# Adaptive-norm FFN on one core: the first token tile in quarters on two queues, fewer matmuls on ones, and one token tile of the second pass two chunks earlier

## What is computed

```python
# x: (32, 64, 1024) f32; weights: (16, 64, 64); w1: (1024, 4096); w2: (4096, 1024)
W = weights[condition]                              # one 64x64 matrix for each of 32 rows
t = einsum('bct,bcd->bdt', x, W)                    # conditioned input, (32, 64, 1024)
h = gelu(einsum('bsd,df->bsf', t, w1) + b1)         # tanh form
out = x + einsum('bsf,fd->bsd', h, w2) + b2
```

## Time and profile before

| | us |
|---|---|
| median of 3 runs (lowest, highest) | 1261.19 (1260.48, 1261.66) |
| the profiled execution | 1260.64 |
| its span | 1258.8 |
| TensorE busy (matmuls) | 1253.7 |
| VectorE busy | 825.6 |
| ScalarE busy | 566.9 |
| GpSimd busy | 188.1 |

### The profile page before, as it was taken

The page is one execution under the profiler, slowest core; times in us unless marked ns, Lnnn a source line. Parts: engine busy times, 40 slices in busy tenths (PEclk is TensorE's granted clock), DMA queues, the critical chain, the costliest instruction groups (busy, mean ns, idle before and its releaser), DMA issues.

```text
span 1258.8 us, 15370 instructions
## 1 busy us (share of the span) xinstructions
PE 1253.7 (100%) x5664; PEld 1043.1 (83%) x5664; DVE 825.6 (66%) x1087; ACT 566.9 (45%) x969; POOL 188.1 (15%) x95
## 2 busy tenths in 40 slices
PE   9999999999999999999999999999999999999998
PEld 9888888888888888888888888888888888888887
DVE  5977787676577777657655455554547767784764
ACT  4845454454544444444434444444444444444442
POOL 4362223321000000000034233312200000000000
PEclk9999999999999999999999999999999999999999
DMA  9586655764997322349835224544189932223431
GB/s 343 160 275 244 242 196 222 283 250 177 384 392 283 97 89 99 101 165 360 310 137 195 95 119 174 184 184 145 74 330 396 351 132 93 101 101 100 155 131 51
DMA packets 94090, 249.28 MB, mean 198 GB/s; under 512 B 7328, under 2 KB 15552, under 8 KB 92608
## 3 DMA queue, kind: packets, MB, share of 16 engines
q1 hardware_dynamic: 93408, 248.14, 54.6%
q10 hardware_dynamic: 576, 0.15, 0.1%
q0 software_dynamic: 32, 0.00, 0.0%
HBM read 162.28 MB, written 85.98 MB: 197 GB/s over the span
## 4 chain that ended last, share of the span: by engine, by line
PE 97%; DVE 1%; DMA 1%; SPq 0%; POOL 0%; ACT 0%; issue 0%; ACTq 0%; DVEq 0%
PE ps L580 48%; PE ps L564 48%; DMA w_raw<-in_L_ffn_inter_w_dram 1%; PE ps L517 1%; POOL s_w L476 0%; SPq L321 0%; DVE y_whole L795 0%; DVE acc L878 0%; DVE lhs L800 0%; DVE y_whole L782 0%; DVE y L789 0%; SPq L318 0%; ACT lhs L646 0%; ACT y_stage L623 0%; SPq L317 0%
## 5 line engine op out<-in xcount | busy, mean ns | idle before, releaser
L564 PE MATMUL ps<-y,lhs 128*128 128x512 f32 x2688 | 611.4, 389 | 0.0
L580 PE MATMUL ps<-rhs,lhs 128*128 128x512 f32 x2688 | 609.6, 389 | 0.0
L580 PEld LDWEIGHTS ps<-rhs,lhs 128*128 128x128 f32 x2688 | 504.7, 188 | 104.6
L564 PEld LDWEIGHTS ps<-y,lhs 128*128 128x128 f32 x2688 | 504.2, 188 | 104.3
L716 ACT ACTIVATE lhs<-h_raw 128x512 fp32r<-128x512 f32 x224 | 141.6, 632 | 345.8 <-PE ps L580 340.2
L859 DVE TENSOR_TENSOR lhs<-h_raw,lhs 128x512 fp32r<-128x512 f32 x224 | 155.0, 692 | 188.5 <-ACT lhs L716 188.5
L800 DVE TENSOR_TENSOR lhs<-w_raw,lhs 128x512 fp32r<-128x512 f32 x128 | 111.1, 870 | 131.6 <-ACT lhs L646 131.5
L646 ACT ACTIVATE lhs<-w_raw 128x512 fp32r<-128x512 f32 x128 | 80.9, 633 | 171.7 <-PE ps L564 165.2
L862 DVE TENSOR_TENSOR rhs<-W,rhs 128x512 fp32r<-128x512 f32 x224 | 153.3, 684 | 0.0
L800 DVE TENSOR_TENSOR lhs<-s_w,lhs 128x512 fp32r<-128x512 f32 x96 | 91.3, 953 | 89.3 <-ACT lhs L646 89.1
L468 POOL TENSOR_TENSOR s_w<-w_raw 128x1024 f32<-128x1024 f32 x16 | 48.9, 3055 | 620.3 <-PE ps L580 354.0
(11 more groups left out here) (38 smaller groups left out, 290.1 us busy)
## 6 DMA issues: line engine op xcount, KB each, us to landing
h_raw<-h_mem SPq DMA_DIRECT2D x112, 512.0 KB, 3.3
w_raw<-in_L_ffn_inter_w_dram SPq DMA_DIRECT2D x32, 1024.0 KB, 8.6
h_mem<-hs SPq DMA_DIRECT2D x64, 512.0 KB, 4.5
W<-in_L_ffn_output_w_dram SPq DMA_DIRECT2D x32, 1024.0 KB, 12.4
h_mem<-c SPq DMA_DIRECT2D x48, 512.0 KB, 5.4
y_mem<-y_out SPq DMA_DIRECT2D x28, 512.0 KB, 3.5
y<-y_mem SPq DMA_DIRECT2D x7, 2048.0 KB, 12.8
acc<-in_x_dram SPq DMA_DIRECT2D x16, 512.0 KB, 9.0
```

The lines of the kernel that those rows point to most:

```text
L564: last = nc.tensor.matmul(ps[:, bank, :], w[:, k, :], y[i][:, part, k, :], start=(i in FRESH and k == 0 and u == 0), stop=(k == KH - 1 and ...
L580: last = nc.tensor.matmul(ps[:, bank2(h, j, tb), :], lhs[s % RING][:, a, blk(tb)], rhs[r][:, w, :], start=(j in FRESH and q == 0 and u == ...
```

## The change

Three things. The first token tile is loaded in four quarters of 256 columns instead of two halves of 512: quarters 0 and 2 are issued by SyncE, 1 and 3 by ScalarE ahead of b1, and TensorE waits for a quarter before every second of the tile's eight matmuls. `WARM` is 13 instead of 15. The eighth token tile of the second pass (j = 7) is multiplied behind chunk 7 instead of chunk 9, and so ScalarE copies it out at chunk 10 instead of 12.

```diff
-    WARM = 15
+    WARM = 13
-        x0_half = sem("x0_half")
+        x0_quarter = [sem(f"x0_quarter{i}") for i in range(4)]
+        def quarter(i):
+            return slice(i * D // 4, (i + 1) * D // 4)
-        BEHIND = (1, 1, 3, 3, 5, 5, 7, 9)
+        BEHIND = (1, 1, 3, 3, 5, 5, 7, 7)
-            sp.dma_start(x0[:, 0, 0:BANK], x_tok[0, :, 0, 0:BANK]).then_inc(x0_half, 16)
-            sp.dma_start(x0[:, 0, BANK:D], x_tok[0, :, 0, BANK:D]).then_inc(x0_in[0], 16)
+            for i in (0, 2):
+                sp.dma_start(x0[:, 0, quarter(i)], x_tok[0, :, 0, quarter(i)]).then_inc(x0_quarter[i], 16)
-                    pe.wait_ge(x0_in[j] if j else x0_half, 16)
+                    if j > 0:
+                        pe.wait_ge(x0_in[j], 16)
-                        if j == 0 and kb == KH:
-                            pe.wait_ge(x0_in[0], 16)
+                        if j == 0 and kb % 2 == 0:
+                            pe.wait_ge(x0_quarter[kb // 2], 16)
             act.dma_start(cond_all[:, SETS // 2:SETS], cond_sets[:, SETS // 2:SETS]).then_inc(cond_in, 16)
+            for i in (1, 3):
+                act.dma_start(x0[:, 0, quarter(i)], x_tok[0, :, 0, quarter(i)]).then_inc(x0_quarter[i], 16)
             act.dma_start(b1_rows[0:F // P], b1.rearrange("(a p) -> a p", p=P)).then_inc(b1_in, 16)
```

## The result

| | us |
|---|---|
| kernel before, median of 6 runs (lowest, highest) | 1261.07 (1260.48, 1261.71) |
| changed kernel, median of 6 runs (lowest, highest) | 1270.81 (1269.45, 1272.01) |
| ratio, with 95% interval | 1.0077 (1.0064 to 1.0089) |
| profiled execution of the changed kernel, its span | 1270.26, 1268.5 |

The change makes the kernel 9.7 us slower, 0.8%. In the profiled executions the spans differ by the same 9.7 us. The result is near the upper end of my range (1264.7 to 1271.0), 2.6 us above the forecast of 1268.2, and close to the first rival, which had the clock fall.

What follows compares the result with a forecast made beforehand. TensorE was taken to bound the kernel. Part 1 counted zero; gaps of 1.83 and 5.18 us before chunks 11 and 12 summed to 7.0, giving 1268.2 us against the median, range 1264.7 to 1271.0.

Steps and rivals of the forecast that it cites:

- first rival: TensorE's clock falls in the new gap, costing 1.7 us more, 1270 in all; chance 0.24.
- Where the time lies: TensorE alone bounds the kernel after 36.79 us; any gap opened there is paid in full.
- Part 1 is zero: Start: quartered first token tile and two fewer matmuls on ones gain nothing; w1 landing moves -0.4 to +0.4 us.
- tile 1 takes a sooner start away: Start: tile 1 has 0.03 us of slack, so a sooner tile 0 is waited away there.
- The wait on the staging store: ScalarE before tile 7's copy: idle some 5.7 us until tile 5's staging DMA lands, copy starting at 64.41.
- The two gaps: TensorE before chunks 11 and 12: 1.83 and 5.18 us lost, 7.0 in sum.
- the row at 93 us: Where both queue, GpSimd's sum goes ahead of VectorE's operation, as at 92.85 and 93.36; VectorE's took 2.88 us.
- The clock: TensorE behind the new gaps: the forecast left the clock unmoved; its fall, priced at 1.7 us, was a rival at 0.24.
- Tile 7's move on TensorE is a pure exchange: Chunks 8 and 9 come 1.7 us later, chunk 10 begins at 63.90 as before, and TensorE waits for nothing.

Runs made afterwards that it cites:

- late copy: The changed kernel with tile 7's matmuls behind chunk 7 but its ScalarE copy at chunk 12 as before; 1264.5 us, ratio 1.0021.
- y6 early: The changed kernel with VectorE making second-pass tile 6's low part before, not behind, its low part for chunk 11; 1262.39 us, ratio 1.0012.
- part 2 alone: The kernel before with only tile 7 of the second pass moved behind chunk 7; 1269.28 us, ratio 1.0065.
- kernel whose clock was held: The changed kernel with 20 idle matmuls, computing nothing used, on TensorE before chunk 12; 1267.7 us, ratio 1.0057.
- later sums: The changed kernel with GpSimd's first sum for w1 group 1 waiting for VectorE's low part for chunk 12; 1266.54 us, ratio 1.0054.
- 10 idle matmuls: The changed kernel with 10 matmuls that compute nothing used on TensorE before chunk 12; 1268.94 us, ratio 1.0067.

## Why the prediction was right, and where it was off

**Where the time lies: right.** TensorE bounds the kernel after 36.8 us, and a gap there is paid in full. The spans differ by what the gaps and the clock make up.

**Part 1 is zero: right in the sum, wrong in the details.** I let tile 0 begin 0 to 0.6 us sooner. In the changed kernel it began at 6.86, not 6.55: 26 records on ones took 5.82 us where 30 had taken 5.16, because the ones ran longer at the slow pace in that execution. In others of this study the 26 took from 4.59 to 5.92. SyncE's first quarter landed 5.0 us after its issue at 1.57, at 6.57, no sooner than the half tile. Nor does tile 0 wait for x and the ones alone, as my working had it: in the late copy and with y6 early it waited 0.4 and 0.5 us for GpSimd's copy into `wdiag`. In the changed kernel nothing of it reached the first stage: chunk 0 began at 21.08, before at 21.05. That tile 1 takes a sooner start away, as I had said, shows in part 2 alone:

```profile
8.75 12.77 PE L500 MATMUL ps<-wdiag,x 128*128 128x128 f32 x112 [0.45 <-DMA x<-in_x_dram]
```

Tile 0 had begun at 6.27 there. In the changed kernel it began late, and TensorE had no wait at tile 1.

**The wait on the staging store: right.** Forecast 64.41, measured 64.56; the store took 8.3 us. Storing it ahead of the load took the whole loss away. ScalarE stood still for 6.15 us where I had some 5.7.

**The two gaps: right.** Forecast 1.8 and 5.2, measured 2.2 and 5.0, sum 7.0 against 7.3; 6.8 by the kernel whose clock was held. GpSimd's sums went ahead of both halves of y6, as I took from the row at 93 us.

**The clock: the step that failed.** I gave the first rival 0.24 and the forecast, with the clock unmoved, 0.50. The clock fell in the profiled execution, and the mean clock of each of the six runs was 0.996 or 0.997 where the kernel before has 1.0. Its price was mis-sized as well: 1.7 us, from the start, against 2.7 to 2.9. Behind the gap TensorE was busy at the lower level for 5.5 us and lost half. The start was a poor measure for that: it scatters, since the 26 records took 4.59 to 5.92 us where 26 x 0.114 = 3.0 would do, 1.6 to 3.0 us more; and it can be read from the pace of the records only, since the granted clock reads 1.00 there in both traces. Of the Trainium skill's rule (TensorE: Matmul & The Clock Gate, HAM oscillation) that waiting brings the clock down, I said that the fall would come in some executions. For the gap of 4.8 us it came in all six. So the 9.7 us are two gaps that I had right and a fall of the clock that I had left to a rival; the range held because it reached as far as that rival.

**Tile 7's move on TensorE is a pure exchange: wrong.** The late copy showed that chunks 8 and 9 coming 1.7 us later leave so little room that y6 can meet GpSimd's sums, and the median goes up by 3 us. In the changed kernel the split for chunk 11 waits longer still for ScalarE, so the forecast didn't suffer.

## What to carry to other kernels

Before moving a step earlier on an engine that works in order, look at the wait that ended last before that step in the trace, and ask whether what it waits for moves too. If it doesn't, everything queued behind the step waits in its stead. Look also at what the delayed work will run beside. Here 6 us of a stalled engine with much spare time cost some 2 us by themselves (an estimate: 1.5 us late in the kernel with later sums, which had 0.8 us less to lose), some 5 more through the sums of GpSimd, and 2.7 more by the clock. A transfer that a wait hangs on belongs ahead of a large load in the same queue: here it landed in 3.9 us ahead of the load and in 8.3 behind it, and issuing the load one store later took the whole loss away.

## What the runs showed of the hardware

TensorE's clock fell to 1.2 GHz (granted 0.50) behind gaps much shorter than the 4.8 us of the changed kernel. In the profiled executions it fell behind gaps of 2.0 us and again 3.2 us (part 2 alone), 2.1 us (y6 early) and 2.55 us (10 idle matmuls). It did not fall behind 2.07 us (the changed kernel's first gap), 2.78 us (the late copy) and 3.13 us (the later sums):

```profile
83.00:86.00 3.00, 3.00 (x13) 1.00 1.02 320
```

The same kernel can go either way: with the late copy and with the later sums the mean clock was 1.0 in some runs and 0.997 to 0.999 in others, and with y6 early it fell in one run of ten. What decides the runs don't show. It stayed low for 3 to 7 us each time.

A 512-column operation of VectorE on two operands in SBUF took 0.68 us alone and 1.3 to 2.4 us where a sum of GpSimd held it. Where both had work queued, GpSimd's sum went first in the changed kernel, and two operations of VectorE beside two sums took 6.69 us and not 2.35.

In the changed kernel a quarter tile issued by ScalarE at 1.52 landed after 3.6 us, one of the same size issued by SyncE at 1.57 only after 5.0. That is no property of the two queues: in the nine profiled executions with quarters ScalarE's took 3.6 to 4.7 us and SyncE's 3.0 to 5.3, and in four of the nine SyncE's was the quicker.
